# Attention row maxima carried in a spare row of masked Q copies, with the last projection in split float32r and one loop per engine

## The chip, the core and the metric

The kernel runs on one core of a Trainium2 chip. The metric is device time in microseconds (us): the whole execution on the device, median of three runs. The core has five engines that work side by side and wait for each other through semaphores: PE (TensorE, matrix multiplication, written to PSUM, which has eight banks), DVE (VectorE), ACT (ScalarE), POOL (GpSimd), and SP (SyncE), which here only issues DMAs. Each engine runs its own instructions strictly in the order in which they are written.

## What is computed

64 sequences of 128 tokens with 256 features pass through two layers. The reference, cut to what matters:

```python
# layer 0: attention with 16 heads of 16 features, relu on the projections
q, k, v = relu(x @ Wq + bq), relu(c @ Wk + bk), relu(c @ Wv + bv)
scores = q_h @ k_h.T / sqrt(16)
scores = where(row mask, scores, 1e-9)
a = softmax(scores, axis=-1)
x = layernorm(a @ v_h + x) * gamma + beta

# layer 1, first half: a Mamba2 block (8 heads of 64, state of 128)
z, xBC, dt = split(rms(x) @ in_proj)
xBC = silu(conv4(xBC)); dt = softplus(dt + dt_bias)
decay = exp(dt * A)            # h = h * decay + (dt*xh) outer B;  y = h . C
u = rms((y + D_skip * xh) * silu(z))
h = x + u @ out_proj

# layer 1, second half: cross attention with 8 heads of 32
q, k, v = ln(h) @ Wq, c @ Wk, c @ Wv
out = h + (softmax(q_h @ k_h.T / sqrt(32)) @ v_h) @ Wo
```

The recurrence over time is computed as a masked product: for each head a 128 x 128 matrix of products of decays is made by a scan, multiplied with B . C, and applied to dt * xh by matmuls.

## The kernel before

The 64 sequences are worked off in 32 groups `g` of two sequences `b` (256 tokens together). A group passes through some 25 kinds of PE steps: `q`, `k`, `v` (the layer-0 projections), `sA`, `tn`, `sT`, `av`, `ot` (its attention), `nt`, `dp`, `cp`, `z` (the in-projection), `bd`, `bx`, `gm`, `y`, `o` (Mamba), `ht`, `q1`, `k1`, `v1`, `sC`, `tC`, `oC`, `wp` (cross attention; `wp` is the output projection). Each step is a small Python function of `(g, i)` that emits its waits and its instructions. Each engine has its own set of such functions, and each engine's order of calls is written out by hand: a long beginning, a loop over the middle groups, and a long end. In the loop five to six groups are under way at once: PE does `q` of group `g+7` in the same pass as `wp` of group `g+2`. The table `USES` gives each PE step its PSUM bank, and through `bank()` the semaphore that says that the bank's last reader is done.

Most projections are computed as "split float32r": a float32 operand is split into a rounded high part and the remainder, and three float32r matmuls (high x low, low x high, high x high) stand for one float32 matmul (`proj3`, L319). A plain float32 matmul shows in the trace as two records.

How layer 0 gets its maxima into the softmax. `sA(g, b)` computes the scores with the query on the rows, four heads beside each other in groups of 32 PE rows, into four banks (8 matmuls of 256 columns). `mA` on DVE reduces each bank to the negated maximum of each row (`sta`, 128 x 16). `nm` and `nw` on DVE (L812, L819) split these into two float32r parts in `NM`; `tn` on PE transposes `NM`; `nt_` on ACT (L1423) copies the result four times with selecting scales into `NT`. `sT(g, b)` then computes the scores again with the keys on the rows: 16 float32 matmuls (L412), and four float32r matmuls of 512 columns (L416) that add `ones @ NT`, that is, the negated maximum of each query. `eA` on ACT takes the exponential. The row mask multiplies Q (`qm` on POOL, L1819; `QM` is loaded from DRAM by `load_m`), so masked rows have scores of zero.

Places that the change touches besides: the output projection `wp` (L669: 4 float32 matmuls of 256 columns, operands `OT` and `wo`); the decay scan `scan` (L977: reads `DB`, writes a single tile `L`) and `lg` (L986, multiplies `L` in place), with `dec_in` on SP loading `DB`; the roots `rs`, `nr`, `hr` on POOL (an addition of EPS and a power of -0.5, on one element per partition, once per sequence) and `hm` on DVE. The `dt` chain runs from `dp` on PE over `d0`, twelve small `dc` steps on DVE and five small steps on ACT to `bd` on PE, then `dk` on DVE, `dec_out` on SP (to DRAM) and `dec_in`.

## Time and profile before

| | |
|---|---|
| median of 3 runs | 1335.6 us (1335.15 to 1338.34) |
| span of the profiled execution | 1337.2 us |
| instructions in the trace | 43414 |
| PE, busy share | 97% |
| PE weight loads, busy share | 86% |
| DVE, busy share | 90% |
| ACT, busy share | 85% |
| POOL, busy share | 69% |
| HBM traffic over the span | 63 GB/s |

The profiled execution's own time was not recorded apart from its span; the span is 1.6 us above the median of the runs and inside their range. A busy share says how much of the span had an instruction of that engine in it. For PE it overstates: the records of matmuls overlap, so the distance between the starts of two matmuls, and not the length of one, is what a matmul costs in a stretch without waits. In the timeline a row with `xN` stands for N instructions merged into one, with the time from the first start to the last end.

### The profile page before, as it was taken

Reading aid. Unit: us, or ns where it says so; the run is one execution under the profiler, and the core shown is the slowest. Engines: PE = TensorE matmul, PEld = TensorE weight load, DVE = VectorE, ACT = ScalarE, POOL = GpSimd, SP = SyncE. Lnnn points to the kernel's source line nnn. Section 1 sums busy time; section 2 is a strip of 40 time slices with the busy share of each in tenths; the row PEclk is TensorE's granted clock in tenths of the full one; section 3 lists DMA queues with packets and bytes.
Section 4 is the critical chain, followed back from the end, with each engine's and each line's share of the span. In section 5 each row is a group of like instructions: output and inputs, shape, how many; then the busy total and the mean of one; then the engine's idle time right before and its main releaser. Section 6 shows DMA issues by size and latency. Waiting matters only on the chain.

```text
span 1337.2 us, 43414 instructions
## 1 busy us (share of the span) xinstructions
PE 1291.6 (97%) x15624; PEld 1148.0 (86%) x15624; DVE 1208.1 (90%) x3056; ACT 1130.8 (85%) x3407; POOL 928.7 (69%) x1200
## 2 busy tenths in 40 slices
PE   5879999999999999999999999999999999999987
PEld 4668889988888998889998889989888898888875
DVE  6789999999999999999999999999999989999982
ACT  5658989888889988888988888998888898888875
POOL 3366777777767777777777776777777777766774
PEclk9889999999999999999999999999999999999999
DMA  6102221212221112222121222211222221111110
GB/s 203 40 34 72 69 77 38 70 56 69 77 77 62 52 49 69 77 77 77 38 66 60 69 77 77 61 53 50 69 77 77 71 71 34 62 56 57 49 57 25
DMA packets 41283, 87.00 MB, mean 65 GB/s; under 512 B 5744, under 2 KB 10992, under 8 KB 41072
## 3 DMA queue, kind: packets, MB, share of 16 engines
q1 hardware_dynamic: 40208, 83.81, 19.7%
q8 instruction: 127, 2.08, 0.6%
q14 instruction: 84, 0.69, 0.2%
q10 hardware_dynamic: 864, 0.42, 0.1%
HBM read 75.53 MB, written 8.68 MB: 63 GB/s over the span
## 4 chain that ended last, share of the span: by engine, by line
PE 87%; DVE 4%; ACT 4%; issue 2%; DMA 1%; POOL 1%; SPq 1%; ACTq 0%; DVEq 0%
PE bank L319 26%; PE bank L422 10%; PE bank L550 6%; PE bank L412 5%; PE bank L379 5%; PE bank L533 5%; PE bank L436 4%; PE bank L564 4%; PE bank L669 4%; PE bank L360 3%; PE bank L604 3%; PE bank L625 2%; PE bank L654 2%; PE bank L470 2%; PE bank L416 1%
## 5 line engine op out<-in xcount | busy, mean ns | idle before, releaser
L951 DVE SCALAR_TENSOR_TENSOR ACC<-bank,cw,ACC 128x250 f32<-128x250 f32 (+2 forms) x576 | 264.1, 462 | 5.9 <-ACT ACC L1535 3.3
L319 PE MATMUL bank<-xnT,wnl 128*128 128x256 f32 x640 | 201.6, 315 | 3.3 <-DVE xnL L883 2.3
L1622 ACT ACTIVATE PC<-bank,stc 128x128 f32<-128x128 f32 x512 | 182.5, 389 | 7.7 <-DVE stc L1068 4.3
L319 PE MATMUL bank<-xnL,wnh 128*128 128x256 f32 x640 | 180.3, 282 | 0.0
L319 PE MATMUL bank<-xnT,wnh 128*128 128x256 f32 x640 | 179.8, 281 | 0.0
L800 DVE TENSOR_REDUCE sta<-bank 128x4 f32<-128x512 f32 x256 | 163.7, 673 | 7.8 <-PE bank L379 7.5
L977 DVE TENSOR_TENSOR_SCAN L<-DB,id 128x1024 f32<-128x1024 f32 x64 | 146.8, 2293 | 0.8 <-DMA DB<-dec_scratch 0.8
L319 PEld LDWEIGHTS bank<-xnT,wnl 128*128 128x128 f32 x640 | 121.9, 190 | 26.0 <-issue 17.6
L1437 ACT ACTIVATE PTA<-bank 128x512 f32<-128x512 f32 x256 | 133.3, 628 | 9.0 <-PE bank L416 5.3
L1916 POOL TENSOR_TENSOR PC<-PC,stc 128x512 f32<-128x512 f32 x128 | 132.1, 1042 | 11.3 <-DVE stc L1075 11.3
L319 PEld LDWEIGHTS bank<-xnL,wnh 128*128 128x128 f32 x640 | 122.4, 191 | 0.0
L319 PEld LDWEIGHTS bank<-xnT,wnh 128*128 128x128 f32 x640 | 121.6, 190 | 0.0
L1871 POOL TENSOR_TENSOR XH<-XH,dtt 128x512 f32<-128x512 f32 x64 | 80.6, 1260 | 56.6 <-ACT XH L1552 56.5
L1622 ACT ACTIVATION_READ_ACCUMULATOR PC<-bank,stc 128x1 f32 x512 | 117.4, 229 | 0.0
L1535 ACT ACTIVATE ACC<-bank,cw 128x256 f32<-128x256 f32 x192 | 109.7, 573 | 8.3 <-PE bank L319 8.2
L1807 POOL TENSOR_TENSOR cL<-cT,cH 128x512 fp32r<-128x512 f32 x31 | 55.8, 1799 | 77.7 <-ACT cH L1372 77.7
L1880 POOL TENSOR_TENSOR Y<-Y,SZ 128x512 f32<-128x512 f32 x64 | 85.8, 1341 | 21.6 <-DVE Y L1011 18.9
L1886 POOL TENSOR_TENSOR Yl<-Y,Yh 128x512 fp32r<-128x512 f32 x64 | 82.6, 1291 | 20.0 <-ACT Yh L1580 19.9
L1423 ACT ACTIVATE NT<-bank,sel 128x128 fp32r<-128x128 f32 x256 | 73.4, 379 | 25.3 <-PE bank L392 25.3
L1636 ACT ACTIVATE PTC<-bank 128x512 f32<-128x512 f32 x128 | 78.6, 620 | 16.6 <-PE bank L422 16.3
L1068 DVE TENSOR_REDUCE stc<-bank 128x4 f32<-128x512 f32 x128 | 84.7, 683 | 7.5 <-PE bank L629 7.5
L1543 ACT ACTIVATE bank<-ACC 128x256 f32<-128x256 f32 x192 | 79.3, 415 | 8.5 <-DVE ACC L951 7.8
(210 smaller groups left out, 4709.9 us busy)
## 6 DMA issues: line engine op xcount, KB each, us to landing
DB<-dec_scratch SPq DMA_DIRECT2D x64, 512.0 KB, 4.0
cT<-in_cT SPq DMA_DIRECT2D x64, 256.0 KB, 2.6
xT<-in_xT SPq DMA_DIRECT2D x32, 256.0 KB, 4.0
xt<-in_xt SPq DMA_DIRECT2D x32, 256.0 KB, 3.8
out_x<-X SPq DMA_DIRECT2D x32, 256.0 KB, 4.0
QM<-qm_rows SPq DMA_DIRECT2D x32, 128.0 KB, 4.1
XC<-in_win SPq DMA_DIRECT2D x2, 644.0 KB, 6.7
PTC<-in_wout SPq DMA_DIRECT2D x2, 256.0 KB, 6.6
```

What stands on the lines that cost most here:

```text
L319: mm = e.matmul(t[:, c0:c0 + T], wt[:, k, m:m + 128], x[:, k, :], start=(n == 0), stop=(n == 5))
L422: mm = e.transpose(t[:, c0 + i * 128:c0 + (i + 1) * 128], src(i), ident[:, :])
L800: e.tensor_reduce(sta[ns % 4][:, 4 * j:4 * j + 4], t[:, :].rearrange("p (i k) -> p i k", i=4), AX_X, ALU.max, negate=True).then_inc(s_mA, 1)
L951: e.scalar_tensor_tensor(out=w, in0=t[:, 0:T].rearrange("p (b t) -> p b t", b=NB)[:, :, 0:125 + k], scalar=cw[:, c, k:k + 1], in1=w, op0=A ...
L977: e.tensor_tensor_scan(L[:, :, :].rearrange("p h t -> p (h t)"), DB[b][:, :], id8[:, :, :].rearrange("p h t -> p (h t)"), 0.0, ALU.mult, A ...
L1068: e.tensor_reduce(stc[g % 4][:, 4 * i:4 * i + 4], t[:, :].rearrange("p (i k) -> p i k", i=4), AX_X, ALU.max, negate=True).then_inc(s_mC, 1)
L1437: e.activation(PTA[n % 4][:, :, :], t[:, :].rearrange("p (i k) -> p i k", i=4), ACT.Exp).then_inc(s_eA, 1)
L1535: e.activation(ACC[n % 3][:, :, :], t[:, 0:T].rearrange("p (b t) -> p b t", b=NB), ACT.Identity, bias=cw[:, c, 4:5], scale=cw[:, c, 3:4]). ...
L1622: op = e.activation(PC[n % 4][:, p, :], t[:, p * 128:(p + 1) * 128], ACT.Exp, bias=stc[g % 4][:, 4 * i + p:4 * i + p + 1], accum_out=stc[g ...
L1880: e.tensor_tensor(cv(Y[:, :]), cv(Y[:, :]), SZ[:, :, b * 128:(b + 1) * 128], ALU.mult).then_inc(s_ga, 1)
L1886: e.tensor_tensor(Yl[:, :], Y[:, :], Yh[:, :].bitcast(F32), ALU.subtract).then_inc(s_yl, 1)
L1916: e.tensor_tensor(PC[n % 4][:, :, :], PC[n % 4][:, :, :], stc[g % 4][:, 16 + 4 * i:20 + 4 * i].unsqueeze(2).to_broadcast([128, 4, 128]), A ...
```

## The change

1. **Maxima in a spare row.** Each 32-row block of Q holds two heads of 16 features. Before there was one Q tile, and the zeros that keep the heads apart were in K alone. Now `qe` on ACT makes two copies of Q (`QT[..][:, m, i, :]`), each with only one head's 16 rows filled (scale `par`), so that 16 rows of each block are spare. K has the value 1 in one spare row (row 16 or 0 of the block, from the bias `kb`, which now adds `sel`). `mA` writes the maxima in a strided order, `tn` transposes `sta` itself (16 columns), `nt_` copies the 16 x 128 result once to `TM`, and a new SP step `put` writes it by DMA (two per sequence, SBUF to SBUF) into the spare rows of Q. The matmuls of `sT` then add the negated maximum by themselves: the four `ones @ NT` matmuls go, and so do `nm` and `nw`. `sT` waits for the DMA (`d_tm`). `sA` has 16 matmuls of 128 columns in place of 8 of 256. `qm` multiplies both copies.
2. **Output projection.** `oT` on ACT writes a rounded `OTh`, a new DVE step `ol` makes `OTl` from the PSUM bank, and `wp` has 12 float32r matmuls in place of 4 float32 ones. The bank of `oC` is free after `ol`. `wo` is loaded to a borrowed tile and split like the other weights.
3. **Scan in place.** `scan` and `lg` work in `DB[b]`; tile `L` goes. `dec_in` waits for the matmuls `y` that read the tile, and no longer for the scan.
4. **Paired roots.** `rs`, `nr`, `hr` and `hm` do both sequences of a group in one instruction, and wait for both.
5. **One loop per engine.** The written-out beginnings and ends go; each engine has one loop from a negative `g` to `NG`, and steps whose group does not exist emit nothing. The orders and the bank table are new.

```diff
 def put(g, b):                                    # SP, new
+    e.wait_ge(s_nt_, 2 * g + b + 1)
+    for i in range(2):
+        e.dma_start(QT[g % 2][16 - 16 * i::32, :, i, b * 128:(b + 1) * 128],
+                    TM[b][8 * i:8 * i + 8, :]).then_inc(d_tm[b], 16)
 def dec_in(g, b):                                 # SP
-        e.wait_ge(s_l, ns - 1)
+        e.wait_ge(s_y, ns - 1)
 def sA(g, b):                                     # PE
-    for m in range(2):
+    for i in range(4):
         for j in range(4):
-            mm = e.matmul(ts[j][:, m * 256:(m + 1) * 256], QT[g % 2][r, m, b * 128:(b + 1) * 128],
-                          KT[g % 2][r, m, b, :, :], start=True, stop=True)
+            mm = e.matmul(ts[j][:, i * 128:(i + 1) * 128], QT[g % 2][r, i // 2, i % 2, b * 128:(b + 1) * 128],
+                          KT[g % 2][r, i // 2, b, i % 2, :], start=True, stop=True)
 def tn(g, b):                                     # PE
-    e.wait_ge(s_nw, ns + 1)
-    e.transpose(t[:, 0:128], NM[ns % 2][:, :, :].rearrange("p j i -> p (j i)").bitcast(F32), ident[:, :])
+    e.wait_ge(s_mA, 4 * ns + 4)
+    e.transpose(t[0:16, 0:128], sta[ns % 4][:, 0:16], ident[:, :])
 def sT(g, b):                                     # PE
-    e.wait_ge(s_nt_, ns + 1)
+    e.wait_ge(d_tm[b], 32 * g + 32)
     ...
-                     QT[g % 2][r, i // 2, b * 128:(b + 1) * 128], start=(i == 0), stop=False)
-    for j in range(4):
-        mm = e.matmul(ts[j][:, :], onesr[r, :], NT[ns % 2][r, :, :].rearrange("p i q -> p (i q)"),
-                      start=False, stop=True)
+                     QT[g % 2][r, i // 2, i % 2, b * 128:(b + 1) * 128], start=True, stop=True)
 def wp(g, i):                                     # PE
-    e.wait_ge(s_oT, g + 1)
+    e.wait_ge(s_ol, g + 1)
     for b in range(NB):
         for kk in range(2):
-            mm = e.matmul(t[:, b * 256:(b + 1) * 256], OT[:, 2 * b + kk, :], wo[:, kk, :], ...)
+            for x, w in ((OTh, wol), (OTl, woh), (OTh, woh)):
+                mm = e.matmul(t[:, b * 256:(b + 1) * 256], x[:, 2 * b + kk, :], w[:, kk, :], ...)
 def scan(g, b):                                   # DVE
-    e.tensor_tensor_scan(L[:, :, :].rearrange("p h t -> p (h t)"), DB[b][:, :],
+    e.tensor_tensor_scan(DB[b][:, :], DB[b][:, :],
                          id8[:, :, :].rearrange("p h t -> p (h t)"), 0.0, ALU.mult, ALU.add)
 def ol(g):                                        # DVE, new
+    e.wait_ge(s_oT, g + 1)
+    e.tensor_tensor(OTl[:, :, :], t[:, :].rearrange("p (k t) -> p k t", k=4), OTh[:, :, :].bitcast(F32),
+                    ALU.subtract).then_inc(s_ol, 1)
 def qe(g, m):                                     # ACT
-    e.activation(QT[g % 2][:, m, :], t[:, 0:T], ACT.Relu, bias=pc[:, m:m + 1])
+    for i in range(2):
+        op = e.activation(QT[g % 2][:, m, i, :], t[:, 0:T], ACT.Relu, bias=qb[:, i, m:m + 1], scale=par[:, i:i + 1])
 def nt_(g, b):                                    # ACT
-    for i in range(4):
-        op = e.activation(NT[ns % 2][:, i, :], t[:, 0:128], ACT.Copy, scale=sel[:, 3 + i:4 + i])
+    e.activation(TM[b][:, :], t[0:16, 0:128], ACT.Copy).then_inc(s_nt_, 1)
 def qm(g, m):                                     # POOL
-    e.tensor_tensor(QT[g % 2][:, m, :], QT[g % 2][:, m, :], QM[g % 2][:, :], ALU.mult)
+    e.tensor_tensor(QT[g % 2][:, m, :, :], QT[g % 2][:, m, :, :],
+                    QM[g % 2][:, :].unsqueeze(1).to_broadcast([128, 2, T]), ALU.mult)
 def rs(g):                                        # POOL; nr, hr and DVE's hm likewise
-    w = sta[ns % 4][:, 33:34]
-    e.wait_ge(s_bg, ns + 1)
+    w = STA[g % 2][:, :, 33:34]
+    e.wait_ge(s_bg, 2 * g + 2)
```

Where the instructions now stand, at three places. First PE around `sT`, in a pass of the loop. `NM` and `STA` hold the maxima, `dts` is the last tile of the `dt` chain (`bd` transposes it), `QT,KT` are the matmuls of `sT`. Before, the steps are `tn(b=0)`, one `cp`, `o`, then `sT(b=0)` (the end of `o` and what follows it):

```order
L552 MATMUL bank<-ones,SQ 128x1
L412 MATMUL bank<-QT,KT 128x128 [waits s_qm,s_sz,s_k2,s_ntc,s_dc,s_f]
L412 MATMUL bank<-QT,KT 128x128 x15
L416 MATMUL bank<-NT,onesr 128x512 x4
L319 MATMUL bank<-xnT,wnl 128x256 [waits s_eC]
```

Now, from the transpose of `b=1` (`tn`) through `sT(b=0)`, one `cp` and the beginning of `o`, and then the end of `o` with `sT(b=1)` and the first `av`:

```order
L394 MATMUL bank<-ident,STA 16x128 [waits s_mA,s_hh]
L412 MATMUL bank<-QT,KT 128x128 [waits s_qm,s_sz,s_k2,s_xc,d_tm0,s_dk]
L412 MATMUL bank<-QT,KT 128x128 x15
L321 MATMUL bank<-xnT,wnl 128x256 [waits s_ntc]
...
L548 MATMUL bank<-ones,SQ 128x1
L412 MATMUL bank<-QT,KT 128x128 [waits s_eA,s_xc,d_tm1]
L412 MATMUL bank<-QT,KT 128x128 x15
L432 MATMUL bank<-PTA,V 32x128 [waits s_eA,s_v]
```

The four `NT,onesr` matmuls are gone; `sT(b=0)` and `sT(b=1)` stand close together, with one `cp` and one `o` between them, and each waits for a DMA (`d_tm0`, `d_tm1`).

Second, SP in a pass of the loop. `cT`, `xT`, `xt` are inputs, `QM` the mask, `decT`, `dec_scratch` and `DB` the decays, `X` the output. Before:

```order
L235 DMA cT<-in_cT 128x512 [waits s_ul,s_cl]
L272 DMA dec_scratch<-decT 16x128 [waits s_dk]
L280 DMA DB<-dec_scratch 128x1024 [waits s_l,d_scr0]
L266 DMA QM<-qm_rows 128x256 [waits s_qm]
L228 DMA xT<-in_xT 128x512 [waits s_xl]
L260 DMA cT<-in_cT 128x512 [waits s_ul,s_cl]
L280 DMA DB<-dec_scratch 128x1024 [waits s_l,d_scr0]
L253 DMA xt<-in_xt 128x512 [waits s_xr]
L286 DMA out_x<-X 128x512 [waits s_f]
```

Now:

```order
L233 DMA xT<-in_xT 128x512 [waits s_xl]
L278 DMA QT<-TM 4x2x128 [waits s_ntc]
L278 DMA QT<-TM 4x2x128
L265 DMA cT<-in_cT 128x512 [waits s_ul,s_cl]
L284 DMA dec_scratch<-decT 16x128 [waits s_dk]
L278 DMA QT<-TM 4x2x128 [waits s_ntc]
L278 DMA QT<-TM 4x2x128
L292 DMA DB<-dec_scratch 128x1024 [waits s_y,d_scr0]
L271 DMA QM<-qm_rows 128x256 [waits s_qm]
L292 DMA DB<-dec_scratch 128x1024 [waits s_y,d_scr0]
L240 DMA cT<-in_cT 128x512 [waits s_ul,s_cl]
```

Four small DMAs (`QT<-TM`) have come in per group; those of `b=1` stand behind the one that stores the decays, which waits for DVE's `dk`.

Third, SP at the start. `PTC`, `HT`, `Q1T`, `OT`, `V`, `K1T` are tiles that are borrowed for weights. Before:

```order
L266 DMA QM<-qm_rows 128x256 [waits s_qm]
L228 DMA xT<-in_xT 128x512 [waits s_xl]
L235 DMA cT<-in_cT 128x512 [waits s_cl]
L244 DMA PTC<-in_wout 128x512 x2
L247 DMA HT<-in_wk 128x512
L247 DMA Q1T<-in_wv 128x512
L247 DMA OT<-in_wq 128x512
L247 DMA wo<-in_wo 128x512
```

Now:

```order
L233 DMA xT<-in_xT 128x512 [waits s_xl]
L278 DMA QT<-TM 4x2x128 [waits s_ntc]
L278 DMA QT<-TM 4x2x128
L278 DMA QT<-TM 4x2x128 [waits s_ntc]
L278 DMA QT<-TM 4x2x128
L271 DMA QM<-qm_rows 128x256 [waits s_qm]
L240 DMA cT<-in_cT 128x512 [waits s_cl]
L249 DMA PTC<-in_wout 128x512 x2
L252 DMA HT<-in_wk 128x512
L252 DMA Q1T<-in_wv 128x512
L252 DMA V<-in_wq 128x512
L252 DMA K1T<-in_wo 128x512
```

The loads of the later weights now stand behind the four `QT<-TM` DMAs of group 0. On ACT, `eA` of group 0 waits for these weights (`d_late`) before its fifth exponential, before and now.

## Rows read from the trace of the kernel before

**Rows 1.** The page's busy line: engine, busy us (share of the span), instructions.
```profile
PE 1291.6 (97%) x15624; PEld 1148.0 (86%) x15624; DVE 1208.1 (90%) x3056; ACT 1130.8 (85%) x3407; POOL 928.7 (69%) x1200
```

**Rows 2.** Busy time by window, as the program fills, and in its middle.
```profile
0.00:100.00 100.00, 72.50 (x712) 61.01 (x713) 76.35 (x181) 57.92 (x139) 40.94 (x64) 0.88 0.29 93
400.00:600.00 200.00, 200.00 (x2488) 179.33 (x2486) 186.10 (x473) 176.74 (x536) 145.37 (x186) 1.00 0.20 65
```

**Rows 3.** Chain of waits, start us, length us: one output projection per group.
```profile
254.35 1.73 PE bank L669 x8
...
1084.55 1.73 PE bank L669 x8
```

**Rows 4.** Timeline of PE: start us, length us, line, op, names, shapes, count.
```profile
649.28 0.28 PE L319 MATMUL bank<-xnT,wnh 128*128 128x256 f32 x1
649.40 1.89 PE L669 MATMUL bank<-wo,OT 128*128 128x256 f32 x8
651.12 0.27 PE L392 MATMUL bank<-ident,NM 128*128 128x128 f32 x1
651.15 0.36 PE L319 MATMUL bank<-xnT,wnl 128*128 128x256 f32 x1
651.35 0.28 PE L319 MATMUL bank<-xnL,wnh 128*128 128x256 f32 x1
...
660.91 1.17 PE L412 MATMUL bank<-QT,KT 32*128 32x128 f32 x32
661.82 0.50 PE L416 MATMUL bank<-NT,onesr 32*128 32x512 f32 x4
662.25 0.66 PE L422 MATMUL bank<-ident,PC 128*128 128x128 f32 x4
...
665.12 1.15 PE L379 MATMUL bank<-KT,QT 32*128 32x256 f32 x16
666.19 0.44 PE L422 MATMUL bank<-ident,xh 128*128 128x128 f32 x2
```

**Rows 5.** Groups by line on DVE, ACT and POOL: busy us, mean ns.
```profile
L1081 DVE TENSOR_TENSOR X<-bank,X 128x512 f32<-128x512 f32 x32 | 22.1, 690 | 25.8 <-PE bank L669 25.8
...
L1423 ACT ACTIVATE NT<-bank,sel 128x128 fp32r<-128x128 f32 x256 | 73.4, 379 | 25.3 <-PE bank L392 25.3
...
L1390 ACT ACTIVATE QT<-bank,pc 128x256 f32<-128x256 f32 x64 | 30.0, 473 | 18.7 <-PE bank L319 18.7
...
L1819 POOL TENSOR_TENSOR QT<-QT,QM 128x256 f32<-128x256 f32 x64 | 47.9, 752 | 19.2 <-DMA QM<-qm_rows 16.1 <-ACT QT L1390 3.1
```

**Rows 6.** Timeline of SP: DMAs issued, the second waits for the first's data.
```profile
656.40 0.33 SPq L272 DMA_DIRECT2D dec_scratch<-decT  x1
658.94 0.33 SPq L280 DMA_DIRECT2D DB<-dec_scratch  x1
```

**Rows 7.** Timeline of DVE: first and last small dt step of one group.
```profile
642.79 0.16 DVE L900 TENSOR_TENSOR dts<-bank,h 128x16 f32<-128x16 f32 x1
...
652.86 0.17 DVE L930 TENSOR_TENSOR dts<-bank,negA 128x16 f32<-128x16 f32 x1 [0.46 <-ACT dtt L1519]
```

**Rows 8.** The start: a transpose on PE, the last weight load, its landing, ACT's wait.
```profile
26.56 0.33 PE L392 MATMUL bank<-ident,NM 128*128 128x128 f32 x1
...
21.29 0.44 SPq L247 DMA_DIRECT2D wo<-in_wo  x1
...
wo<-in_wo SPq DMA_DIRECT2D x1, 256.0 KB, 6.8
...
34.48 2.06 ACT L1437 ACTIVATE PTA<-bank 128x512 f32<-128x512 f32 x4 [3.69 <-PE bank L416]
```

**Rows 9.** Timeline of PE: the transposes of xn, groups 0, 1 and 31.
```profile
45.47 0.84 PE L422 MATMUL bank<-ident,xn 128*128 128x128 f32 x4 [0.75 <-ACT V L1413]
...
84.96 0.74 PE L422 MATMUL bank<-ident,xn 128*128 128x128 f32 x4 [1.23 <-ACT xn L1471]
...
1265.37 0.74 PE L422 MATMUL bank<-ident,xn 128*128 128x128 f32 x4
```

More of the change, by code:

```diff
@@ L1055, in kk1 @@
                         e.wait_ge(s_sC, g)
+                    if m == 0 and g == 0:
+                        e.wait_ge(z_1l, 3)
                     e.wait_ge(s_k1p, 2 * g + m + 1)
@@ L1987, in gpsimd @@
-            lo_u(NG - 1); r2(NG - 1, 1); hr(NG - 1, 0); hr(NG - 1, 1); nC(NG - 2, 2); nC(NG - 2, 3); nC(NG - 1, 0)
-            nC(NG - 1, 1); nC(NG - 1, 2); nC(NG - 1, 3)
+            for g in range(-5, NG):
+                r2(g + 1, 1)
+                nC(g, 3)
+                hr(g + 1)
+                lo_x(g + 5)
+                xr(g + 3, 0)
+                lo_c(g + 5)
+                dx(g + 2, 0)
+                xr(g + 3, 1)
+                xd(g + 2, 0)
+                rs(g + 3)
+                nr(g + 3)
+                ga(g + 2, 0)
+                xd(g + 2, 1)
+                dx(g + 2, 1)
+                s2_(g + 2, 0)
+                yl(g + 2, 0)
+                nC(g + 1, 0)
+                qm(g + 5, 0)
+                ga(g + 2, 1)
+                r2(g + 2, 0)
+                yl(g + 2, 1)
+                s2_(g + 2, 1)
+                qm(g + 5, 1)
+                lo_u(g + 2)
+                nC(g + 1, 1)
+                nC(g + 1, 2)
@@ L2030 @@
         "par": np.stack([(p // 16 + 1) % 2, (p // 16) % 2], 1).astype(np.float32),
-        "sel": np.stack([p % 32 == i for i in range(3)] + [(p % 32 < 8) & (p % 4 == i) for i in range(4)], 1).astype(np.float32),
+        "sel": np.stack([p % 32 == i for i in (0, 1, 2, 16, 0)], 1).astype(np.float32),
         "pcols": pcols,
```

913 lines of the change are left out of this document (297 added, 616 removed), and 22 rows, old and new, of the table USES.

## The prediction

> **What bounds the kernel now.** I read the page's busy line first, then the windows, the chain of waits, the timeline of PE, and last the groups by line. PE is busy 97% of the span, DVE 90%, ACT 85%, POOL 69% [rows 1]. The windows say where the missing 3% lie: in the first 100 us PE is busy for 72.5, and from 400 to 600 for all 200, while DVE has 186.1, ACT 176.7 and POOL 145.4 [rows 2]. So in the middle PE is the bound, with DVE 7% behind. The chain of waits there consists of PE alone, and one output projection after the other stands in it at a fixed distance: 1084.55 - 254.35 = 830.2 us for 21 groups, 39.5 us per group [rows 3]. A PE instruction taken out of a pass is worth its distance in the timeline, as long as nothing else becomes late. The fill and the drain go by other rules. The transposes of xn (`nt`) start at 45.5, 85.0 and, for group 31, 1265.4 us [rows 9]: a head of 45.5 us, 31 intervals of 39.35 us, and a tail of 1337.2 - 1265.4 = 71.8 us. The first interval is already 39.5 us long although PE has idle time there, so a chain of several engines has that length too.
>
> **PE, per group.** All prices are distances between starts.
>
> `sT`: it starts at 660.91, its `NT` matmuls at 661.82 and the next step at 662.25 [rows 4], so it takes 1.34 us, 0.43 of them the part that goes. But the 32-row matmuls must drain before a full-height one can follow. `sA` has the same amount of float32 columns and no such tail, and takes 666.19 - 665.12 = 1.07 us [rows 4]. I take 1.34 - 1.07 = 0.27 us saved, at most 0.43, twice per group: 0.54 (up to 0.86).
>
> `sA` gets 16 matmuls of 128 columns for 8 of 256, the same columns. The 32 records of `sT` take 0.91 us up to the next start, against 1.07 for `sA` with a drain [rows 4]. Between 0 and 0.16 us saved each; I take 0. `tn` has 0.03 us up to the next step [rows 4] and stays.
>
> `wp`: now 651.12 - 649.40 = 1.72 us for eight records. The float32r matmuls of 256 columns are 649.40 - 649.28 = 0.12 us apart, and a first one after float32 work is 651.35 - 651.15 = 0.20 apart from the next [rows 4]. Twelve of them: 12 x 0.12 = 1.44, plus 0.08 for the switch, 1.52 us. Saved: 0.2 us. (Their length of 0.28 us would make it 3.4 us and a loss of 1.7; the distances of the same matmuls exclude that.)
>
> The new order of the loop: I count 13 places before, and 11 now, where float32r work follows float32 work, at 0.08 us each. 0.16 us saved, with 0 and 0.3 as ends.
>
> Sum: 0.54 + 0.20 + 0.16 = 0.9 us; the longer ends make 0.86 + 0.32 + 0.2 + 0.3 = 1.7 us, the shorter 0.6 us. I take 1.0, as one of two `sA` gains of 0.16 is likely: 38.5 us per group. Of the 31 intervals the first three and the last are not PE's. 27 x 1.0 = 27 us.
>
> **The other engines** must do a group in 38.5 us. DVE uses 186.1 / 200 x 39.5 = 36.8 us of a group [rows 2]. It loses two `nm` and two `nw`, small steps of about 0.17 us as those of `dt` are [rows 7], and one `hm`, no cheaper, and gets `ol`, which reads a bank of 128 x 512 as `fin` does, 0.69 us [rows 5]: about 36.7 us, 95% of 38.5. ACT: 34.9 us. Eight copies into `NT` of 0.29 each (73.4 / 256) become two; `qe` doubles, two more activations of 0.47 [rows 5]: 34.9 - 1.7 + 0.9 = 34.1 us. POOL: 28.7 us; `qm` at most doubles, + 1.5 [rows 5]; three pairs of roots become one each, which saves more than 1 us. All fit, so no engine overtakes PE, but DVE keeps only 2 us of slack per group, and its dependences get tighter.
>
> **The waits that are added.** `sT(b=1)` now waits for `put`. Behind it on PE stands everything, so a late arrival costs its full lateness. After `tn(b=1)` PE does `sT(b=0)`, one `cp` and one `o` before it: 1.07 + 6 x 0.12 + 0.08 + 12 x 0.12 + 0.2 = 3.5 us. In that time must pass: the transpose, 0.27 us long [rows 4], and its handover to ACT, 0.35; the copy, at most 0.38 [rows 5]; two issues on SP of 0.33, of which the first counts in full; and the flight. For the flight the nearest rows are the store of the decays at 656.40 and the load that waits for it at 658.94, 2.54 us including the first issue [rows 6]. Sum: 0.35 + 0.38 + 0.33 + 2.54 = 3.6 us. So it is late by about 0.1 us, if ACT and SP are free at once. 27 x 0.1 = 3 us; bounds 0 and 1.0 us per group. `sT(b=0)` has some ten us more and doesn't wait. The Trainium skill (DMA: Bandwidth & Descriptors, Anatomy of one DMA) gives a fixed cost of about 2.0 us per transfer, measured on the other issuing path; with it the put would arrive at 3.1 us, and the 3 us would go. The trace's 2.54 us, which holds the issue as well, nearly agrees.
>
> `o(b=0)` now waits for `ol` (its bank was that of `oC`). `ol` stands on DVE right ahead of the `dc` steps, about 5 us of PE work after `oC`. I cost it at nothing; DVE's slack is the cover.
>
> **The head.** In the trace the last weight load is issued at 21.29 and lands 6.8 us later, at 28.1; the fifth exponential starts at 34.48, after a wait for PE [rows 8]. So the weights were no limit. Now their loads stand behind `put(0,1)`, thus behind both transposes of group 0. In the trace the second of these is at 26.56 [rows 8], and as much work stands ahead of it now; then the copy, two puts and the mask load (2 us) and six weight issues (4.5 us) pass before `wo` is issued, near 33.5, and with 6.8 us of flight `wo` lands a little after 40. Three weight copies on ACT follow (1.6 us). The fifth exponential starts near 42 in place of 34.5, and with it all that hangs on sequence 1 of group 0, `nt` of group 0 last. + 8 us, with 0 (if the chain after it has room) and 13 as ends.
>
> **The tail.** `ol` comes between `oT` and `wp` (0.7 us and a handover) at the very end; the order there is the loop's own, with `bx` ahead of work that was ready. + 2 us, 0 to 7.
>
> **Sum.** 1337.2 - 27 + 3 + 8 + 2 = 1323.2 us of span. The median of the runs lies 1.6 us below the profiled span: 1322 us.
>
> **Rivals.**
>
> *The put stalls every pass.* The mechanism: on SP the puts of `b=1` stand behind `dec_out`, which waits for DVE's `dk`, and `dk` for `bd`, one `cp` ahead of `tn(b=1)` on PE. If `dk` comes 1 us after the copy to `TM`, or the flight takes 3.5 us, `sT(b=1)` is 1.1 us late in each of 27 groups: + 30 us in place of 3, 1349 us, slower than before. It decides from (1335.6 - 1322) / 27 = 0.5 us beyond my 0.1. For it: two engines and a queue must all be free at once, and DVE is 95% full. Against it: SP itself is idle at this point, and `bd` comes 0.9 us ahead of `tn`. The Trainium skill's same page adds that any wait of a DMA is made on the issuing sequencer, before dispatch; it holds for this rival that nothing overtakes a waiting `dec_out`. No row here shows such a wait in front of an urgent transfer.
>
> *The `dt` chain becomes the bound.* `d0` to the last `dc` step took 652.86 - 642.79 = 10.1 us [rows 7], with other DVE work between. On PE there lie now `dp` (eight matmuls of at most 0.12), four blocks of six float32r matmuls, `y` (priced as `sA`), `o`, `wp` and `z` ahead of `bd`: 0.9 + 2.9 + 1.1 + 1.6 + 1.5 + 1.4 = 9.4 us. DVE has 27 instructions from `d0` to the last `dc`: 14 small ones of 0.17, and 13 others at its mean of 186.1 / 473 = 0.39 us [rows 2], 7.5 us. Add `dp` itself and three handovers of some 0.3, and it is 9.3, just what there is. If DVE enters this stretch 0.5 us late in every pass, half the gain goes: 1322 + 13 = 1335 us, no change. For it: `d0` follows directly on a PE step. Against: DVE has 2 us of slack per group to catch up.
>
> *The head costs nothing and the drain is as before.* In the trace even the intervals with an idle PE take 39.5 us, so a late fifth exponential could be made up by shorter first intervals. 1322 - 10 = 1312 us. Against it: sequence 1 of group 0 heads the only chain that is under way there.
>
> *The change doesn't do what it says*: PE could keep 39.5 us if the matmuls of `sT` don't drain sooner without the `NT` part. Then only `wp` and the order remain, 10 us less gain: 1332 us.
>
> **Chances.** My forecast 0.55; the put 0.15 (1349); the `dt` chain 0.12 (1335); the free head 0.13 (1312); the missing drain 0.05 (1332). A measurement of this kernel can tell 0.3% from no change, 4 us: 1331.6 to 1339.6. Faster: nearly all of the forecast (0.52), the free head (0.13), a third of the chain's and the drain's cases (0.06), and a small part of the put's (0.03), 0.74. Same: 0.03 + 0.06 + 0.01, 0.10. Slower: 0.11 of the put, 0.03 of the chain, 0.02 of my forecast's edge, 0.16. The range must take in the free head with the longer ends of PE's sum (27 x 0.4 = 11 us below 1312, of which I take most) and most of the put: 1303 to 1346 us.
>
> **What would show it.** In the new profile: output projections 38.5 us apart in the middle; `sT` of 1.07 us with no `onesr` record; `wp` of 1.5 us in twelve records; PE still busy for 199 of 200 us from 400 to 600. `sT` released by DMA `QT<-TM`, in sum below 5 us for the first case and near 30 for the put's; `bd` released by ACT's `dts`, near zero for mine. The `nt` of group 0 near 53 us. The forecast is wrong if PE's wait for the puts or for `bd` exceeds 0.5 us per group, or if the distance of the projections isn't below 39.

## The result and the profile after

The changed kernel takes 1378.95 us (median of 4 runs, 1377.57 to 1382.6), the kernel before, run beside it, 1335.72. The ratio is 1.0321, with a 95% interval of 1.0304 to 1.0338: slower by 3.2%. The forecast was 1322 us with a range of 1303 to 1346, so it missed in sign and in size.

The page's busy line of the changed kernel (engine, busy us, share of the span, instructions) and its windows (busy us of PE, PEld, DVE, ACT, POOL with counts, then PE's granted clock, the DMA share, GB/s):

```profile
PE 1292.5 (94%) x16520; PEld 1177.2 (86%) x16520; DVE 1198.6 (87%) x2930; ACT 1102.8 (80%) x3280; POOL 971.5 (71%) x1007
```
```profile
0.00:100.00 100.00, 62.73 (x671) 55.49 (x675) 54.40 (x140) 49.02 (x109) 29.48 (x41) 0.80 0.28 89
...
400.00:600.00 200.00, 198.59 (x2635) 182.29 (x2638) 186.82 (x459) 172.44 (x515) 155.36 (x158) 1.00 0.21 68
```

Against [rows 1, 2] two things are to be seen. The first 100 us hold 10 us less work of PE, 22 less of DVE, and the mean granted clock there is 0.80 in place of 0.88. And in the middle PE now has 1.4 us of gaps in 200 us, where it had none. PE's busy sum has not fallen, though work was taken out: a matmul's record goes on until its modelled end, so short waits hide in it.

The span of the changed kernel is 1375.8 us. The transposes of xn cut it in three, as in [rows 9]:

```profile
64.55 0.60 PE L418 MATMUL bank<-ident,xn 128*128 128x128 f32 x4
...
104.50 0.60 PE L418 MATMUL bank<-ident,xn 128*128 128x128 f32 x4
...
1294.85 0.75 PE L418 MATMUL bank<-ident,xn 128*128 128x128 f32 x4 [2.49 <-ACT xn L1299]
```

| us | before | forecast | after | best of any variant (runs 10, 9 and 1) |
|---|---|---|---|---|
| head, to `nt` of group 0 | 45.5 | 53 | 64.5 | 48.2 |
| 31 intervals, each | 39.35 | 38.6 | 39.69 | 38.94 |
| drain, from the last `nt` | 71.8 | 74 | 80.9 | 77.5 |

So the 38.6 us between the two spans are 19.1 in the head, 31 x 0.335 = 10.4 in the middle and 9.1 in the drain. Each of the three was forecast better than that. (The medians lie 43.2 us apart. A run's time is 1.8 us more than its span, so the profiled execution of the kernel before took about 1339.0 us, 3.3 over its median; that of the changed kernel took 1377.57, 1.4 under its own.)

**The middle, step by step.** I took the distance from each PE step's start to the next one's start over all passes from 400 to 1200 us, and for each step its shortest and its mean. Before, a pass is 39.48 us in most passes and no step waits. After, the passes run from 39.02 to 41.63 us, with a mean of 39.8. (The shortest distances of all steps sum to 38.7 us, but no pass reaches that: the best one, 39.02, is the measure.) Of the 0.8 us between the best pass and the mean, nearly all stand at four places: `sA(0)` (1.39 us in the mean, 1.10 at best), `gm(1)` (0.44, 0.31), `ht(1)` (0.42, 0.30) and `k1(0)` with its neighbours `tC` and `av` (0.23 over the best). One pass shows the first. SP's queue, then POOL, DVE and PE (the bracket is the idle time before, and what ended it):

```profile
633.89 0.33 SPq L284 DMA_DIRECT2D dec_scratch<-decT  x1
634.69 1.11 SPq L278 DMA_DIRECT2D QT<-TM  x2
637.03 0.33 SPq L292 DMA_DIRECT2D DB<-dec_scratch  x1
637.41 0.43 SPq L271 DMA_DIRECT2D QM<-qm_rows  x1
637.94 0.38 SPq L292 DMA_DIRECT2D DB<-dec_scratch  x1
638.41 0.38 SPq L240 DMA_DIRECT2D cT<-in_cT  x1
638.84 0.42 SPq L298 DMA_DIRECT2D out_x<-X  x1
639.32 0.48 SPq L258 DMA_DIRECT2D xt<-in_xt  x1
```
```profile
647.97 0.73 POOL L1589 TENSOR_TENSOR xa<-xa,xt 128x256 f32<-128x256 f32 x1 [3.17 <-DMA xt<-in_xt]
```
```profile
648.74 0.43 DVE L769 BATCH_NORM_STATS2 STA<-xa 128x6 f32<-128x256 f32 x1 [1.38 <-POOL xa L1589]
...
649.77 1.21 DVE L906 TENSOR_TENSOR DB<-DB,bank 128x1024 f32<-128x1024 f32 x1
```
```profile
651.03 1.17 PE L381 MATMUL bank<-KT,QT 32*128 32x128 f32 x32 [0.61 <-DVE DB L906]
```

Read it from below. PE's `sA(0)` waits for `lg` on DVE, which frees its bank; `lg` waits for nothing itself, but is queued behind `bn_stats`; that waits for POOL's residual add, and this for `xt`. The `xt` load is the last of six transfers, 1.97 MB, that SP issues within 2.8 us. All of them stand behind `put(1)` in its fixed order, and behind the first load of `DB`, which waits until the store of the decays (`dec_scratch`, 633.89) has landed. The kernel before spreads the same traffic over its pass:

```profile
619.90 0.34 SPq L280 DMA_DIRECT2D DB<-dec_scratch  x1
620.28 0.43 SPq L266 DMA_DIRECT2D QM<-qm_rows  x1
620.76 0.43 SPq L228 DMA_DIRECT2D xT<-in_xT  x1
628.68 0.33 SPq L260 DMA_DIRECT2D cT<-in_cT  x1
629.11 0.38 SPq L280 DMA_DIRECT2D DB<-dec_scratch  x1
630.38 0.33 SPq L253 DMA_DIRECT2D xt<-in_xt  x1
```
```profile
660.85 0.73 POOL L1835 TENSOR_TENSOR xa<-xa,xt 128x256 f32<-128x256 f32 x1
```

There `xt` was issued 30 us ahead of its use. After, it is used 8.7 us after its issue and waited for. The median flights, from the page's part on DMA issues (size, us from issue to landing), were 3.8 for `xt` and 4.0 for `DB` before:

```profile
DB<-dec_scratch SPq DMA_DIRECT2D x64, 512.0 KB, 5.2
...
xt<-in_xt SPq DMA_DIRECT2D x32, 256.0 KB, 7.6
```

The Trainium skill (DMA: Bandwidth & Descriptors, Where 436 GB/s comes from) puts the limit between HBM and SBUF near 358 GB/s; an estimate by it for the bunch is 1.97 MB / 358 GB/s = 5.5 us, plus the fixed 2 us that the same page gives (Anatomy of one DMA, for the other issuing path), 7.5 us in all. The trace does not agree: the bunch, issued from 637.03 on, is waited for until 647.97, 10.9 us. From 637 to 648 the mean is 204 GB/s, with 408 in the best whole microsecond and 36 in the one from 640 to 641. So the limit does not explain how long the bunch takes, and what does is open:

```profile
637.00:648.00 11.00, 10.55 (x158) 9.46 (x157) 9.28 (x22) 8.98 (x20) 4.31 (x7) 1.00 0.58 204
```

**The head.** ACT's rows around the fifth exponential, against [rows 8]:

```profile
35.19 2.07 ACT L1265 ACTIVATE PTA<-bank 128x512 f32<-128x512 f32 x4 [2.42 <-PE bank L412]
43.92 0.63 ACT L1263 ACTIVATE wk1h<-HT 128x512 fp32r<-128x512 f32 x1 [6.67 <-DMA K1T<-in_wo]
...
45.50 1.06 ACT L1265 ACTIVATE PTA<-bank 128x512 f32<-128x512 f32 x2
...
47.89 0.66 ACT L1185 ACTIVATE xH<-xT 128x512 fp32r<-128x512 f32 x1
```

The fifth exponential comes at 45.5, not 42, and 11 us after that of before. The first one, though, is 11 us late as well, before ACT waits for any of these weights; with the weights early (run 2) the fifth comes at 37.8. So both the late start and the weights are in the 45.5. And `split_x(2)`, which before ran at 23.48, ahead of it, stands behind it in the loop's order, and so does the rest. In the kernel before:

```profile
23.48 0.63 ACT L1359 ACTIVATE xH<-xT 128x512 fp32r<-128x512 f32 x1 [0.63 <-DMA xT<-in_xT]
24.01 2.04 ACT L1437 ACTIVATE PTA<-bank 128x512 f32<-128x512 f32 x4
```

### The profile page after: what moved, and what is told of

It reads as the page before. It is cut to its first block and busy times, and to the rows that moved or that the text cites. A ratio compares the mean times of both kernels' runs of the same rounds, so it can differ in the third digit from the quotient of the medians.

```text
span 1375.8 us, 44888 instructions
## 1 busy us (share of the span) xinstructions
PE 1292.5 (94%) x16520; PEld 1177.2 (86%) x16520; DVE 1198.6 (87%) x2930; ACT 1102.8 (80%) x3280; POOL 971.5 (71%) x1007
## 5 line engine op out<-in xcount | busy, mean ns | idle before, releaser
L321 PE MATMUL bank<-xnT,wnl 128*128 128x256 f32 x640 | 198.0, 309 | 1.8 <-DVE X L948 1.8
L740 DVE TENSOR_REDUCE STA<-bank 128x4 f32<-128x512 f32 x256 | 166.8, 685 | 32.0 <-PE bank L381 31.8
L1265 ACT ACTIVATE PTA<-bank 128x512 f32<-128x512 f32 x256 | 142.6, 597 | 30.1 <-PE bank L432 23.2
L897 DVE TENSOR_TENSOR_SCAN DB<-DB,id 128x1024 f32<-128x1024 f32 x64 | 147.7, 2308 | 3.8 <-DMA DB<-dec_scratch 3.6
L321 PEld LDWEIGHTS bank<-xnT,wnl 128*128 128x128 f32 x640 | 121.0, 189 | 17.5 <-issue 11.5
L1623 POOL TENSOR_TENSOR XH<-XH,dtt 128x512 f32<-128x512 f32 x64 | 114.6, 1791 | 17.6 <-ACT XH L1380 17.6
L1231 ACT ACTIVATE KT<-bank,kb,par 128x256 f32<-128x256 f32 x128 | 65.4, 562 | 59.2 <-PE bank L321 59.0
L1603 POOL TENSOR_SCALAR STN<-STN 128x2 f32<-128x2 f32 x32 | 7.6, 236 | 138.4 <-ACT junk L1288 138.4
L1572 POOL TENSOR_TENSOR QT<-QT,QM 128x512 f32<-128x512 f32 x64 | 82.4, 1289 | 12.7 <-DMA QM<-qm_rows 11.0
L1632 POOL TENSOR_TENSOR Y<-Y,SZ 128x512 f32<-128x512 f32 x64 | 82.6, 1290 | 8.3 <-DVE Y L931 8.2
L381 PE MATMUL bank<-KT,QT 32*128 32x128 f32 x2048 | 77.9, 290 | 11.0 <-DVE STA L740 5.6
```

The costliest lines, as they stand in the source:

```text
L321: mm = e.matmul(t[:, c0:c0 + T], wt[:, k, m:m + 128], x[:, k, :], start=(n == 0), stop=(n == 5))
L740: e.tensor_reduce(sta[ns % 4][:, 0:16].rearrange("p (e j m) -> p j m e", e=2, j=4)[:, j], t[:, :].rearrange("p (m e k) -> p m e k", m=2, e ...
L897: e.tensor_tensor_scan(DB[b][:, :], DB[b][:, :], id8[:, :, :].rearrange("p h t -> p (h t)"), 0.0, ALU.mult, ALU.add).then_inc(s_l, 1)
L1265: e.activation(PTA[n % 4][:, :, :], t[:, :].rearrange("p (i k) -> p i k", i=4), ACT.Exp).then_inc(s_eA, 1)
L1623: e.tensor_tensor(hv(XH[0][:, :]), hv(XH[0][:, :]), dtt[g % 3][:, b * 8:b * 8 + 8].unsqueeze(2).to_broadcast([128, 8, 64]), ALU.mult).then ...
L1632: e.tensor_tensor(cv(Y[:, :]), cv(Y[:, :]), SZ[:, :, b * 128:(b + 1) * 128], ALU.mult).then_inc(s_ga, 1)
```

## The experiments

Each kernel is an edit of the changed one, but for the burst (6), which is one of the kernel before. Times are medians; the kernel before took 1337.1 to 1338.5 us beside them.

**1. `xt` early.**
```diff
                 load_x(g + 7)
+                load_t(g + 5)
                 put(g + 5, 0)
...
                 store(g)
-                load_t(g + 5)
```


> One edit of the changed kernel: on SP the load of `xt` is issued right behind the load of `xT`, ahead of both puts, and no longer last in the bunch behind put(b=1). Theory A (the middle gave its gain back to a late `xt`): in the changed kernel a pass has 38.7 us of PE work by the shortest distances and 1.1 us of waits at k1(0), ht(1), sA(0) and gm(1); POOL waits 1.4 us per pass for the load of xt, DVE's bn_stats 0.8 us for POOL, and PE for what DVE does then. With xt early these go: 38.8 us per pass, -28 us, about 1350 us. Theory B (DVE, 93% full, is the reason, whatever xt does): the pass stays near 39.8 us and the time near 1377 us. Theory C (ACT and POOL chains through XH, which is a single buffer, are the reason): also no change, and PE's wait for XH stays.

1368.6 us (ratio 1.0231, 1.0203 to 1.0259), -10 us. POOL's wait for `xt` (27.3 us from 400 to 1200) and DVE's for POOL (16.0) are gone, and so are PE's at `ht(1)`, `sA(0)` and `gm(1)`. The best pass, 39.02 us, is now frequent, but passes of 39.9 to 41.3 remain. Theory A holds for the steady waits and not for its 28 us. The longest pass, 41.33 us, ACT and PE:

```profile
958.26 0.63 ACT L1198 ACTIVATE cH<-cT 128x512 fp32r<-128x512 f32 x1 [2.30 <-DMA cT<-in_cT]
```
```profile
955.24 1.07 PE L432 MATMUL bank<-PTA,V 128*32 128x128 f32 x31
957.83 0.27 PE L432 MATMUL bank<-PTA,V 128*32 128x128 f32 x1 [1.51 <-issue]
```

The next load of the same bunch, `cT`, is late by up to 2.3 us on ACT (10.9 us in ten passes). But it is not what this pass lost on PE: PE stops inside one step, ahead of the last matmul of `av(7)`, where no semaphore stands, and the four `av` of `b=1` take 2.78 us in place of 1.01, 1.77 of the 2.3 us that the pass is over the best. The 19 passes from 400 to 1200 us are 10.0 us over 19 x 39.02, and four stops of this kind make 4.5 of them. In another long pass (39.97 us) PE waits 0.71 us for `xa` on DVE, which is queued behind a scan that has waited 1.04 us for `DB`. So two things are left: late data, and stops with no releaser.

**2. Weight loads early, 3. no `ol`.**
```diff
 load_x:  e.dma_start(xT[:, :, :], a["xT"][g])
+         if g == 2: ... the six weight loads, moved here from load_c
```


> One edit of the changed kernel: the six weight loads of the third block stand on SP right behind the load of xT for group 2, ahead of put(0,0), as they stood before the change. Theory A (the head's 19 us come from these loads: ACT's copies wait for them, and the fifth exponential, split_x(2) and q(2) behind the copies): fifth exponential back near 35 us, nt of group 0 from 64.5 to 54 us, -10 us in all, 1369 us. Theory B (the head is long because one loop order fills the pipeline badly, with the weights only one of many waits): nt of group 0 no earlier than 60 us, less than 5 us gained, 1375 us or more.


```diff
 ol:  e.wait_ge(s_oT, g + 1)
-     e.tensor_tensor(OTl, bank, OTh, ALU.subtract)
 wp:
-     for x, w in ((OTh, wol), (OTl, woh), (OTh, woh)):
+     for x, w in ((OTh, wol), (OTh, woh), (OTh, woh)):
```


> The changed kernel without the DVE instruction that makes the low part of the split output (0.69 us per group); the output projection reads the high part in its place, with as many matmuls, so this part of the computation is wrong. Theory B (DVE's fullness sets the pass): 0.7 us less in each of about 28 passes, -20 us, 1359 us. Theory A (a late xt does): DVE has more slack but starts bn_stats no earlier: under 5 us gained, 1374 to 1379 us.

Weights early: 1375.6 us, the time of theory B; `nt` of group 0 at 57.0, between the two theories. So 7.5 of the head's 19 us were the weights, but the middle happened to be longer (31 intervals of 40.0, the waits for `xt` and `cT` as before) and took half of it back. Without `ol`: 1380.5 us, no gain. DVE's busy time from 400 to 600 fell from 186.8 to 182.1 us and the waits for `xt` stayed at 27.2: a DVE with less to do does not help where a load is late.

**4. The queue spread out, 5. with weights early and one edit of the drain, 6. a useless burst before the change.**
```diff
                 load_x(g + 7)
+                load_m(g + 7)
+                store(g)
+                load_t(g + 5)
+                load_u(g + 3)
                 put(g + 5, 0)
-                load_u(g + 3)
                 dec_out(g + 4)
                 put(g + 5, 1)
                 dec_in(g + 4, 0)
-                load_m(g + 7)
                 dec_in(g + 4, 1)
                 load_c(g + 7)
-                store(g)
-                load_t(g + 5)
```


> The changed kernel with another order of SP's queue alone: load_x, load_m, store, load_t, load_u, and then put(0), dec_out, put(1), two dec_in, load_c. Four transfers (QM 128 KB, the output, xt and the second cT, 256 KB each) leave the bunch behind put(1); 1.28 MB of 1.9 MB stay. The run with xt alone moved early lost its steady waits at ht, sA and gm (best passes 39.02 us), but kept irregular ones of up to 1.8 us, at av, k1 and tC, which come while the bunch is in flight, some inside a step where no semaphore stands (0.7 to 1.05 us between two matmuls of one projection, against 0.12). Theory A (the supply of instructions, itself by DMA, waits behind the bunch): these irregular waits shrink with the bunch, passes of 39.0 to 39.3 us, 1354 to 1360 us. Theory B (they come from something else on PE or its order): no change against the run with xt early, 1368 us.


```diff
 scalar:
+                if g == NG - 3: yh(g + 2, 1); qq(g + 2, 1)
                 eC(g + 1, 2)
...
+                if g == NG - 2: he(g + 1, 0); he(g + 1, 1)
                 pC(g, 2)
```


> The queue's order of the run before, and with it the weight loads early (nt of group 0 came 7.5 us sooner in the run that had this alone) and one edit of the drain: on ACT yh and qq of (31,1) ahead of the last two exponentials of group 30, and both he of group 31 ahead of the last two pC of group 30. Theory A (the drain's 9 us are ACT's loop order): o(31,1) comes 3 us sooner and q1 of group 31 another 1.4; with the head that is -11 us against the run with the order alone. Theory B (the drain is set by DVE and PE, ACT's order only stands beside it): the drain stays at 81 us, -7 us from the head alone.


```diff
 (kernel before)  store(g)
+                for i in range(4):
+                    e.dma_start(spare[g, i], a["xT"][g]...).then_inc(d_sp, 16)
```


> The kernel before the change with four useless transfers of 256 KB each per loop pass (memory to memory, nobody waits for them) behind all of the pass's own loads on SP. Theory A (instructions are late when a bunch is in flight): matmuls of one step come up to 1 us apart, without a semaphore between them, which the kernel before never shows; 0.3 to 1 us more in each of 23 passes, 1343 to 1360 us. Theory B (only data that somebody waits for counts): the loads behind the bunch have slack, no change, 1336 to 1340 us.

Spread: 1354.8 us (1.0123, 1.0099 to 1.0146), -24 us against the changed kernel, and inside theory A's 1354 to 1360. 15 of 20 passes take 39.0 us, the mean is 39.12, 31 intervals 38.95 each. The one edit of the queue's order returns (39.69 - 38.95) x 31 = 23 us.

The burst: 1336.9 us, no change (0.9995, 0.9981 to 1.0008), though 1 MB more flew in each pass, and no matmul of a step was late in its trace between 400 and 1200 us. So the theory that a bunch by itself makes instructions late failed in this kernel, where nothing in the queue is urgent.

It is not refuted for the changed kernel, and the packets kept in the traces speak for it. The page lists a queue of instructions beside those of data:

```profile
q8 instruction: 134, 2.20, 0.6%
```

Between 400 and 1200 us PE stops inside a step for over 0.4 us, with no semaphore there, three times in the changed kernel and four times in run 1, each time some 8 us after the issue of the last `DB`, in passes that lie five or ten apart. All seven stops end 1.3 to 1.5 us after the end of a 16 KB packet of this queue. These seven packets start 16.4 to 18.0 us after the one before, and they are the only ones of the two traces there that do (the median is 9 us). In the spread kernel the longest such distance is 16.2 us, and there is no stop. This is a match of times, seven out of seven, and no experiment; no run separates these stops from the late data, as both went with the same edit. Their share is 2.2 of the 15.2 us that the changed kernel's 19 passes are over the best one.

The drain's edit: 1351.3 us, 3.5 less than the spread kernel, and the two traces do not say from where. The head is 2.6 us shorter (`nt` of group 0 at 59.6, from 62.2), but the next intervals give that back (`nt` of group 3 at 177.5, from 176.8), and the drain gave nothing (80.6 us, from 80.3). Theory B for the drain.

**7. The fill, 8. two transposes moved.**
```diff
 scalar:  split_x(1) ahead of ve(0); weight copies ahead of e.wait_ge(s_av, ...)
          wouth copies behind n1(0, 1)
 gpsimd:  wk1l, wv1l, wol behind xr(0, 1), not ahead of it
```


> The kernel with the queue spread, weights early and the ACT edit of the drain (1351 us, nt of group 0 at 59.6 us), plus four edits of the fill alone: split_x(1) ahead of the first V copy on ACT (3 us), the three subtractions for the weights' low parts behind the second residual add on POOL in place of ahead of it (3.8 us, DVE waited 3.0 for it), the four wouth copies behind n1(0,1) on ACT (1.7), the three weight copies ahead of the wait for av (1.6). Theory A (the head is a chain through all engines, and what one loop order puts in front of it counts in full): nt of group 0 near 49 to 51 us, -9 us, 1342 us. Theory B (the chain has other links beside these: DVE's mA and the banks): nt stays past 56 us, 1348 us or more.


```diff
                 bx(g + 2, 1)
+                tn(g + 4, 0)
                 v(g + 5, 0)
                 nt(g + 3, 0)
-                tn(g + 4, 0)
...
                 k(g + 5, 1)
+                tn(g + 4, 1)
                 cp(g + 3, 2); bd(g + 3, 0); cp(g + 3, 3)
-                tn(g + 4, 1)
```


> The same base, with two transposes moved on PE alone: tn(0) from between nt and sC to ahead of v, tn(1) from ahead of sT(0) to ahead of cp(2). In the changed kernel a tn costs 0.20 us to the next start with float32 matmuls behind it, and before the change 0.03 with a float32r projection behind it. Theory A (what a small float32 step costs is set by the kind of its successor): 0.17 + 0.17 saved less 0.08 for bx, which now has tn behind it; undisturbed passes of 38.76 in place of 39.02 us, -8 us, 1343 us. Theory B (a step's cost moves with its position, and the sum of a pass stays): 39.02 us and 1351 us.

The fill: `nt` of group 0 at 53.1, 6.5 us sooner and between the two theories, but 1348.0 us, the time of theory B, as the middle was 0.13 longer per interval.

The transposes: 1352.6 us, theory B. The rows of PE in the changed kernel, and with the move:

```profile
660.89 0.60 PE L418 MATMUL bank<-ident,xn 128*128 128x128 f32 x4
661.33 0.27 PE L394 MATMUL bank<-ident,STA 128*16 128x128 f32 x1
661.53 1.17 PE L621 MATMUL bank<-K1T,Q1T 32*128 32x128 f32 x32
```
```profile
643.33 0.60 PE L418 MATMUL bank<-ident,XC 128*128 128x128 f32 x4
643.76 0.27 PE L394 MATMUL bank<-ident,STA 128*16 128x128 f32 x1
643.79 0.48 PE L357 MATMUL bank<-vbias,onesr 128*128 128x512 f32 x1
...
645.54 0.60 PE L418 MATMUL bank<-ident,xn 128*128 128x128 f32 x4
646.07 1.17 PE L621 MATMUL bank<-K1T,Q1T 32*128 32x128 f32 x32
```

`tn` takes 0.20 us up to `sC` and 0.03 up to `v`. But then `bx(1)` takes 0.43 in place of 0.36, `nt` 0.53 in place of 0.44, and the projections around `tn(1)` 0.16 more: the two `tn` fell by 0.34 us, the others rose by 0.33, and the best pass is 39.01 us in place of 39.02. At these two places the small step did not get cheaper; its neighbours paid.

**9. All together, 10. fill and drain again, 11. `cT` ahead of `DB(1)`.**
```diff
 9:   7 and 8; vector: lg(31, 1) ahead of mC(30, 0); gpsimd: r2(31, 1) behind s2_(31, 1)
 10:  7 without 8; gpsimd: wk1l, wv1l, wol behind nr(0); lg, r2 as in 9, hr(31) behind r2(31, 1)
 11:  10; sync: load_c(g + 7) ahead of dec_in(g + 4, 1)
```


> The fill's four edits, the two moved transposes and two more edits of the drain (DVE: lg(31,1) ahead of the maxima of group 30; POOL: the root r2(31,1) behind s2(31,1), ahead of lo_u and of two nC), together. Theory A: -9 and -8 as above and -3 of the drain, 1331 us, faster than the kernel before the change by 0.4%. Theory B: not below 1338 us.

> The run with the queue spread and the four edits of the fill (1348 us; nt of group 0 at 53.1 us, drain 81.8 us), with two more findings of its trace and of the one with everything together. Fill: POOL's three subtractions for the weights' low parts (4.2 us) now stand in front of the root of the first norm; they go behind the second root. Drain: POOL's roots r2(31,1) and hr(31) stand behind lo_u and up to three nC (DVE waited 4.2 us for hr); they go right behind s2(31,1), and lg(31,1) ahead of group 30's maxima on DVE. Theory A (fill and drain are one chain through all engines, and each instruction of the loop's order that stands in it counts in full): nt of group 0 near 50 us, drain near 77 us, -7 us, 1341 us or less. Theory B (the chain only moves to the next engine, as when the two edits of ACT's drain order gave nothing): nt past 52 us, drain past 80 us, 1346 us or more.

> The kernel of the run beside it, with load_c ahead of dec_in(b=1) on SP, so that fewer bytes fly with DB of b=0. What is left of irregular waits in these traces is about 0.4 us in every fifth pass, where DVE's scan waits for DB of b=0. Theory A (late loads are all that is left between 39.02 us and the mean of 39.1): every pass 39.02, 2 us less than the run beside it. Theory B (each fifth pass has another reason): no change.

1345.2, 1342.9 (1.0037, 1.0024 to 1.005) and 1347.8 us. The first is theory B's, not below 1338. The second is the best of all variants, and still slower than the kernel before. Its head is 48.2 us, 16.4 less than the changed kernel's, better than theory A had it. The fill's edits were made together, so what each is worth isn't shown, but for the weights (run 2) and for POOL's subtractions behind the root, which are all that was changed in the fill since run 7 (4.9 us). The third was neither theory's: 4.9 us slower than the second, in place of 2 faster or the same. The second's drain went to 80.0 only, theory B: `o(31, 1)` came 46.5 us after the last `nt`, from 48.0, then the next step of group 31 waited for another root or subtraction on POOL. What is left there is a chain through five engines, and I did not find its order.

**12. The scan late, 13. and behind `kk1`.** What the best variant still loses in the middle (39.24 in place of 39.02) are passes in which DVE's scan waits 0.6 to 1.2 us for `DB`. The traces show why, and it is not the flight of `DB`, 3.8 to 4.4 us in these five passes as in the others: it is the store of the decays ahead of it, which lands 3.4 to 3.6 us after its issue in place of 1.35, so that `DB` is issued 1.5 us late. These passes too lie four or five apart. Why the store is late there is not shown.
```diff
 12 (and in the drain hr(31) behind lo_u):
                 tap(g + 3, 14)
-                scan(g + 3, 0)
...
                 xc(g + 3, 5)
+                scan(g + 3, 0)
                 kk1(g + 2, 0)
 13: the last two lines exchanged
```


> The kernel with the queue spread and the edits of fill and drain (1343 us; passes of 39.02 us, but single ones of 39.5 to 40.1, mean 39.24), with one edit of the loop: on DVE scan(b=0) stands behind the last xc, in place of ahead of tap 15, so DB may land 3 to 4 us later; and in the drain the root hr(31) behind lo_u, not ahead of it. In the irregular passes DVE's scan waited 0.4 to 1.0 us for DB, with the taps, the reciprocal and xa queued behind it, and PE's ot waited for xa. Theory A (a load that DVE needs just in time is what is left of the loss): nearly all passes 39.0 us, -6 us, 1336 us, level with the kernel before the change. Theory B (the scan's new place makes lg, which frees a bank for sA, late in every pass: DVE has only 5% of slack): passes of 39.2 us or more, no gain, 1343 us or more.

> The kernel of the run before (scan(b=0) late on DVE: every pass 40.79 us, all irregular waits gone, but PE's ot(1) waits 1.7 us in each pass for the bank that kk1(0) frees, and kk1 stands behind the scan of 2.2 us), with these two instructions exchanged: kk1(0), then scan(0). Theory A (each wait in the loop is one instruction's place on DVE against one deadline; with DB given 3 us more and kk1 back ahead of the scan nothing is late): every pass 39.0 us, 1397 - 31 x 1.77 = 1342 us, and with the drain's roots in better order 1337 us. Theory B (some 2 us of DVE work have to stand in front of one deadline or another, so that the wait only moves, to sA behind lg): 39.3 to 40.3 us per pass, 1350 to 1380 us.

1397.1 and 1427.3 us (1.0448 and 1.065). The long passes of the one kind are gone in both, and in both another wait has come, in every pass. The waits from 400 to 1200 us (engine, line, waited for: sum, times, longest), first of the one, then of the other:

```profile
PEld bank L418 <- DVE K1T L978: 35.9, 20, 1.8
PE bank L418 <- DVE K1T L978: 31.2, 20, 1.6
```
```profile
PEld bank L381 <- DVE DB L906: 37.0, 19, 2.0
PE bank L381 <- DVE DB L906: 32.5, 19, 1.7
```

With the scan ahead of `kk1`, PE's `ot(1)` waits for the bank that `kk1` frees, and every pass is 40.79 us. With `kk1` ahead, `lg` comes late behind the scan, `sA(0)` waits for it, and a pass is 41.3 us or more. (In five of the 18 passes it is 42.8 us.) Theory B's direction in both, but not its account: in the first it had named `lg` as late, and it was `kk1`, and in the second its 1350 to 1380 us were too little. Of the three places tried, only the first lets nothing wait for the scan of 2.2 us, and there it starts 4.7 us after the issue of its `DB`, whose flight in run 10 is 4.2 us in the median and 4.5 at most.

## Why the prediction was wrong

*PE's work per group.* "Sum: ... I take 1.0": measured 0.46 (39.48 to 39.02, in passes where nothing is late). By step, distances summed over a pass: `sT` -0.47 (2.68 to 2.21; forecast -0.54), `wp` -0.21 (1.72 to 1.51, in twelve records; forecast -0.20). These two terms were right. `sA` cost 0.06 more (forecast 0 to 0.3 less), and the rest of the order 0.16 more, not 0.16 less: `tn` +0.21, `ot` +0.25 and `ht` +0.12, `bx` -0.17, `av` -0.12, all projections together -0.13. I had priced "`tn` has 0.03 us up to the next step and stays" by its successor of before, and by one of two: the other `tn` of a pass already took 0.16 us before, with a `tC` behind it. Run 8 shows what a moved transpose does: its 0.17 turns up at the neighbours. Counting the switches between the two kinds of matmul at 0.08 each was a price that no row had isolated, and the count was off as well: the trace has 14 such places before, two of them inside `sT`, and 11 after, where I had 13 and 11.

*27 us of gain.* This is the step that failed most. "All fit, so no engine overtakes PE": true of the busy sums (DVE is at 93% in the middle), and beside the point. The new order of SP's queue, with six transfers behind a put and a store that wait for the end of a pass, I read only for what the put would do. The load that became late was none that the change speaks of. Runs 1 and 4 show it: 23 us come back with the order of the queue alone, late data and PE's stops together. So the middle is +10.4 us as built, and -12.3 us (31 x 0.397) with the loads in time, against -24 forecast.

*The put's wait, + 3 us.* It is 0: `sT` takes 1.10 us up to the next start for either `b` in the steady passes. PE waits for the transfer once, in the fill:

```profile
31.40 0.27 PE L394 MATMUL bank<-ident,STA 128*16 128x128 f32 x1
33.04 2.09 PE L412 MATMUL bank<-QT,KT 32*128 32x128 f32 x32 [1.37 <-DMA QT<-TM]
```

Its two DMAs were issued at 30.56 and 31.27, so issues and flight together took 2.5 us, and the second DMA under 1.8 from the start of its issue. I had taken 2.54 for one issue and the flight, from a pair that goes through DRAM, and one issue besides. The Trainium skill (DMA: Bandwidth & Descriptors, Anatomy of one DMA) with its 2.0 us was nearer, and would have removed this term; the measured 1.8 is a little below it.

*`o(b=0)` and `ol` at nothing:* right, as no `o` waits in the steady passes, and leaving `ol` out gains nothing.

*The head, + 8 us.* It is + 19.1. The mechanism was there, with 3.5 us too little for it: the step "as much work stands ahead of it now" put the second transpose of group 0 at 26.56, and it starts at 31.40. With these loads out of the way (run 2) 11.5 of the 19.1 us remain. What was missing is that one loop per engine puts independent work in a fixed line behind it: `split_x(2)` behind the weight copies, POOL's three subtractions (3.8 us) ahead of the residual add, the `wouth` copies ahead of the norm. The fill's edits, with the weights early and the queue spread, took out 16.4 of the 19.1 us. The mean clock granted to PE over the first 100 us was 0.80, against 0.88 before and 0.88 again in run 10; whether it cost time or only followed PE's idle stretches is not shown.

*The tail, + 2 us.* It is + 9.1, beyond my 7. Two attempts to shorten it by an engine's order left it at 80.6 and 80.0 us. That can't be told from scatter: in runs 1 to 11 the drain takes 77.5 to 82.1 us, and the 77.5 is run 1's, which does not touch it. So the place of the 9 us is not shown; the landmarks are only these: `y(31, 0)` came 27.0 us after the last `nt` before and 31.8 after, `q1` of group 31 50.1 and 59.2, the end 71.8 and 80.9.

*The rivals.* The put did not stall, and the `dt` chain did not bound: `bd` waited 4.1 us in the whole span. The free head was wrong in sign, and nothing was made up: the first three intervals took 117.1 us before and 117.1 after. The missing drain was wrong too: `sT` takes 1.10 us in place of 1.34 without its `NT` part. The one that came was in none: the queue's order, not its puts. Its sign was in a sentence of the first rival, that nothing overtakes a waiting transfer on SP. I applied it to the put and not to the six transfers behind it.
